# The value products of an attention group issued in one or two bursts in place of three parts

## The reference, cut to what matters

```
sim  = einsum('bhid,bjd->bhij', q, k) * SCALE + attn_bias
sim  = where(causal or masked, -big, sim)
attn = softmax(sim, axis=-1)
out  = einsum('bhij,bjd->bhid', attn, v)      # the value products
out  = ln(out.reshape(b, n, H * DH) @ Wout, g_out)
```

## Time and profile before

| | |
|---|---|
| median of 3 runs | 2250.94 us (2246.36 to 2251.7) |
| span of the profiled execution | 2243.8 us |
| difference of the two | 7.1 us |
| PE busy | 1965.3 us, 88% |
| DVE busy | 1693.1 us, 75% |
| ACT busy | 1338.8 us, 60% |
| POOL busy | 1085.5 us, 48% |

### The profile page before, as it was taken

How to read it: one execution, slowest core, us unless ns; L and a number is a source line. 1 busy time by engine, 2 the same in 40 slices (tenths; PEclk the granted TensorE clock), 3 DMA queues, 4 the chain that set the end, 5 groups by cost and what they waited for, 6 DMA issues and landing times. The chain is left out here.

```text
span 2243.8 us, 46782 instructions
## 1 busy us (share of the span) xinstructions
PE 1965.3 (88%) x11698; PEld 1421.4 (63%) x11698; DVE 1693.1 (75%) x4092; ACT 1338.8 (60%) x2911; POOL 1085.5 (48%) x1307
## 2 busy tenths in 40 slices
PE   5999585999999998589999999985796999999988
PEld 4887463666666668566666666675564666666658
DVE  4777867877887785758777877758577888877857
ACT  2222665777776674247676767644565777766754
POOL 0443222666765562306666666623034666666643
PEclk8999697999999999799999999997896999999999
DMA  4630166333333343286777888830464433333333
GB/s 118 203 109 31 42 226 250 104 113 113 113 114 113 106 149 110 82 312 189 236 241 236 244 244 243 271 142 21 148 229 163 131 115 116 108 115 107 107 113 113
DMA packets 220535, 338.75 MB, mean 151 GB/s; under 512 B 25766, under 2 KB 102700, under 8 KB 220364
## 3 DMA queue, kind: packets, MB, share of 16 engines
q1 hardware_dynamic: 220364, 336.85, 47.3%
HBM read 250.62 MB, written 102.91 MB: 158 GB/s over the span
## 5 line engine op out<-in xcount | busy, mean ns | idle before, releaser
L1653 POOL TENSOR_SCALAR at_row<-at_row,at_inv 128x129 f32<-128x129 f32 (+7 forms) x384 | 715.2, 1862 | 352.9 <-DVE at_inv L1817 347.2
L1864 ACT ACTIVATE at_row<-at_row,at_nmax 128x129 f32<-128x129 f32 (+7 forms) x768 | 595.4, 775 | 231.8 <-DVE at_nmax L1836 230.2
L1836 DVE CUSTOM_DVE_ANT_0 at_row<-at_s,bias,at_row 128x128 f32<-128x128 f32 (+7 forms) x768 | 617.8, 810 | 63.3 <-PE at_s L1764 35.9
L1776 PE MATMUL at_t<-ident,at_row 128*128 128x128 f32 x3456 | 543.9, 280 | 42.6 <-ACT at_pt L1857 37.7
L1776 PEld LDWEIGHTS at_t<-ident,at_row 128*128 128x128 f32 x3456 | 391.4, 141 | 247.9 <-issue 165.7
L1763 PE MATMUL at_s<-k_hh,q_hl 128*128 128x512 f32 (+3 forms) x1152 | 462.2, 401 | 41.9 <-SPq L1721 21.8
L1792 PE MATMUL at_o<-at_pt,v 128*64 128x512 f32 (+3 forms) x2304 | 438.9, 503 | 5.8 <-ACT at_pt L1857 2.5
L1668 DVE COPY at_pt<-at_t 128x128 f32<-128x128 f32 (+3 forms) x576 | 278.5, 484 | 179.6 <-PE at_t L1776 175.7
L1764 PE MATMUL at_s<-k_lp,q_h 65*128 65x512 f32 (+3 forms) x1152 | 392.9, 353 | 0.0
L1857 ACT ACTIVATE at_pt<-at_t 128x512 f32<-128x512 f32 (+2 forms) x576 | 306.7, 533 | 135.5 <-PE at_t L1776 130.3
L1763 PEld LDWEIGHTS at_s<-k_hh,q_hl 128*128 128x128 f32 x1152 | 224.6, 195 | 76.1 <-DVE at_nmax L1836 32.2
(11 more groups left out here) (249 smaller groups left out, 2863.9 us busy)
## 6 DMA issues: line engine op xcount, KB each, us to landing
q_hl<-q_dram SPq DMA_DIRECT2D x192, 256.0 KB, 4.0
q_dram<-o_in SPq DMA_DIRECT2D x76, 512.0 KB, 3.7
bias<-bands_dram SPq DMA_DIRECT2D x64, 512.0 KB, 5.4
q_h<-q_dram SPq DMA_DIRECT2D x96, 256.0 KB, 4.8
o_dram<-o_sb SPq DMA_DIRECT2D x96, 256.0 KB, 4.3
bands_dram<-brow_dram SPq DMA_DIRECT2D x2, 8192.0 KB, 33.6
bias<-corners_dram SPq DMA_DIRECT2D x256, 64.0 KB, 4.2
bias<-in_fside SPq DMA_DIRECT2D x32, 448.0 KB, 4.8
```

The costliest lines, as they stand in the source:

```text
L1653: return eng.tensor_scalar(cells, cells, inv[:, i:i + 1], None, ALU.mult)
L1776: last = eng.transpose(t_ps[m % NTR][:, c * P:(c + 1) * P], row[:, u % RING, here:here + P], t["ident"][:])
L1836: eng.tensor_tensor_reduce(out=row[:, u % RING, ZERO:ZERO + width], in0=s_ps[u % 2][:, 0:width], in1=bt[:, lo:lo + width], scale=-1.0, sca ...
L1864: eng.activation(cells, cells, ACT.Exp, scale=-1.0, bias=nmax[:, i:i + 1], accum_out=rsum[:, i:i + 1]).then_inc(s["exp"], 1)
```

## The change

The steps at which V stands now depend on the parity of the group. An early group's products are issued in one burst at u % 8 = 1. A late group's are issued in two, at u % 8 = 0 and 3, with 8 products each. The step of O follows the last part by one, as it did before.

```diff
-    VALUES_AT = (0, 2, 4)
+    VALUES_AT = ((1,), (0, 3))
@@ values
-                    n = len(VALUES_AT)
+                    n = len(VALUES_AT[g % 2])
@@ TensorE step
                     g = u // GU - 1
-                    if u % GU in VALUES_AT and has(g, NGRP):
-                        values(turn, g, VALUES_AT.index(u % GU))
+                    if u % GU in VALUES_AT[g % 2] and has(g, NGRP):
+                        values(turn, g, VALUES_AT[g % 2].index(u % GU))
@@ ScalarE step
-                    g, part = divmod(n - LAG - VALUES_AT[-1] - 1 - GU, GU)
-                    if part == 0 and has(g, NGRP):
+                    u = n - LAG
+                    g = u // GU - 1
+                    if u % GU == VALUES_AT[g % 2][-1] + 1 and has(g, NGRP):
                         output(turn, g)
```

## The result

The changed kernel took 2308.1 us, the median of 4 runs (2306.52 to 2311.12), against 2249.35 (2246.36 to 2251.7) for the kernel before beside it: a ratio of 1.0258, with a 95% interval of 1.0239 to 1.0277. It is 58.75 us slower. The forecast was 29 us slower, and the time lies 2 us above its range. The direction was right and the size was half.

The account below looks back on a forecast made before the run. TensorE was taken to bound only parts of the period, VectorE being late from A(10) on. 48 periods x (29.1 - 28.49) = +29 us gave span 2273; adding 7.1 to reach the median of the runs gave 2280 us, range 2232 to 2306.

Parts of the forecast that it names:

- Fewer switches: On TensorE, three value-product parts fewer a period at 0.3 us each: 0.9 us saved if TensorE is the bound throughout.
- VectorE's chain: VectorE's additions and scalings from A(10) on: A(13) starts at 16.84, not 15.92, so VectorE is 0.9 us later.
- TensorE's pace: Rival: TensorE sets the pace throughout, 2208 us, or 2231 with half given back; chance 0.22.
- The late group's second burst delays A(10); N(8) meets GpSimd: Behind L(9): VectorE's A(10) starts at 10.76, not 9.35; its scaling N(8) ends at 13.2, not 12.8.
- The early burst delays T(10) and X(15): Behind L(15): T(10) starts at 21.45, not 18.29; ScalarE's X(15) at 22.61, not 20.64, with O ahead of it.
- N(14): "I take 29.1": VectorE's scaling near the period's end: period 29.33 us if slow, 28.9 if quick, 29.1 taken.
- The ordinary period: The schedule laid out from a period without disturbance, 27.92 us before: 29.33 us if N(14) is slow.
- Loop and layer 2: Periods with the loop's branch or layer 2's query wait: waits covered except some 0.45 us; 29.1 taken, between 28.5 and 29.8.
- rival on the clock: Rival: new stands at L(13) to L(15) lower TensorE's clock in each of 24 turns, +36 on top, 2316 us; chance 0.04.
- The sum: Whole kernel: 48 x (29.1 - 28.49) = +29 us, predicted time 2280 us.
- all slow and the branch not covered: Rival: 29.8 us in every period, +63, 2314 us; chance 0.06.
- The page's lock: Rival: at N(14) GpSimd's port lock fully blocks VectorE, twenty-four at 1.2 us, +29 on top, 2309 us; chance 0.02.

Follow-up runs that it names:

- two and two: Kernel before, with two bursts per group: the late group's at 0 and 4, the early group's at 0 and 2; 2229.72 us, ratio 0.9893.
- the short N(9): Changed kernel, with GpSimd's scaling N(9) cut from 641 columns to 129 in every period; 2289.24 us, ratio 1.017.
- 129-column N(15): Changed kernel, with GpSimd's scaling N(15) cut from 1025 columns to 129 in every period; 2274.65 us, ratio 1.0109.

## Why the prediction was half right

- *Fewer switches, 0.9 us a period of TensorE.* Not borne out. The group of the value products is busy 0.76 a period less, but TensorE's whole busy time fell by 3.7 us, 0.08 a period (the rest was overlap counted in two groups). With two and two, two parts fewer, it fell by 15.3 us, 0.16 a part and not 0.3. The forecast didn't rest on this term, since it took VectorE's chain for the limit, and that was right: TensorE's pace as a rival falls with 91% busy and 111.8 us of waits ahead of the logits. Where the parts are fewer and the chain isn't delayed (two and two) the ordinary period of layer 3 is 0.42 shorter.
- *The late group's second burst delays A(10); N(8) meets GpSimd.* Right: 10.81 against 10.76, and N(8) ends at 13.25 against 13.2. Moving that burst by one step gave back 49 us; taking away N(8)'s meeting alone (the short N(9)) gave back 18.
- *The early burst delays T(10) and X(15).* Right in its times. The text lets O stand at the head of ScalarE's queue, and it does; but O one step later brought only 0.1 for X(15), so the hold is T(10) behind the burst.
- *N(14): "I take 29.1".* **This is the step that failed: the length of the period, taken as 29.1 and measured as 29.76 on average.** The mechanism was right and this term too small, in three parts, of which N(14) is one and the next two points are the others. The text gave 29.33 if slow and 28.9 if quick, and the forecast went half way between. The schedule itself had N(14) 0.05 behind GpSimd's start, and the earlier trace rows have a slow one at 0.03 behind. It had to be taken as slow. Measured, it is 0.14 behind in most periods and slow in 42 of 48, and the two cases lie 0.5 apart in the kernel before, near the forecast's 0.43. Taking 29.33 would have added 0.23 x 48 = 11 us.
- *The ordinary period.* With N(14) slow it was forecast at 29.33; the ordinary ones have a mean of 29.58. Steps of 0.05 to 0.12 that add up to T(13), and some periods that are longer still, make 0.25, another 12 us over 48 periods.
- *"Loop and layer 2 … for these I take 29.1 too".* The turn-first periods have a mean of 29.94 (before 29.17), 0.36 above the ordinary ones, which is 0.18 over all. The text itself left some 0.45 of the branch uncovered and then took 29.1 for these periods too, so it put that at nothing. The wait for queries did go, as forecast, and with it layer 2's stretches at the lower clock. Nearly all of the excess lies in the six periods with a stop ahead of C(8), and most of it in two of layer 1, of 32.06 and 31.91 us. In these two, in both kernels, N(12) meets GpSimd's N(13) and takes 1.45 in place of 0.70; in the changed kernel T(12) then starts 1.2 to 1.4 later than in the other two of layer 1 with the stop, and the granted clock is at the lower level (0.50) for 3.4 us. The clock of that layer is 0.99 in the windows, where it was 1.00. That is part of the rival on the clock, at two places in place of 24. Why the clock fell only there stays open.
- *The sum.* 0.23 + 0.25 + 0.18 = 0.66 us a period over 29.1, 32 us in 48. The medians differ by 58.75 and the spans by 65.5: the span of the change's profiled execution lies 1.2 us above the median time, that of before 5.6 below, so that the rows show some 7 us more than the runs.
- *The rival "all slow and the branch not covered".* It came nearest, with 29.8 a period and 2314 us, and had a chance of 0.06. The N(14) are slow in 42 of 48, and the turn-first periods are 0.36 longer, near the 0.45 that the text had left uncovered, though nearly all of it lies in six of them.
- *The page's lock.* By the rule in the Trainium skill's page SBUF — State Buffer (section SBUF: two separate sides), that the loser of the shared port fully blocks for the whole instruction, N(14) would not have ended before 2.9 us behind GpSimd's start. It ended 1.66 behind, so the trace goes against this form of the rule, and the rival built on it falls. What it says of a conflict between the two engines is borne out: with GpSimd's instruction cut short, N(14) took 0.78.

How the 59 us are made up is shown by the runs with parts: 19 for the early burst and 26 for the late ones by themselves, some 14 only for both. In the changed kernel the second late burst at its step is worth 49, of which N(8)'s meeting is 18; that the other 31 are A(10)'s late start by itself is argued from the times in the table, and no run shows it alone.

## What to carry to other kernels

Merging parts of an engine's work can save its switches only where that engine sets the pace, and the saving is read from the engine's whole busy time, not from that of one group: look at what the next engine waits for behind each place, and put a long burst where its follower has slack. Where a schedule laid out by hand ends in a case of two outcomes, take the outcome that its own start times select, not the middle. Whether VectorE or GpSimd pays for a conflict can hang on the difference of two start times (0.028 and 0.030 us here), so count how often it falls each way over all periods, before and after, rather than reading one.

## What the runs showed of the hardware

- **VectorE behind GpSimd is held for a fixed share, and released before GpSimd is done.** Over the 96 periods of the two kernels, N(14) takes 0.74 to 0.76 us wherever it starts from 0.21 ahead of GpSimd's N(15) to 0.028 behind it, and GpSimd's then takes 3.30 to 3.46 in place of 2.90. From 0.030 to 0.22 behind it takes 1.44 to 1.63, and ends 1.66 behind GpSimd's start each time, whether it started 0.05, 0.14 or 0.22 behind. (Of four starts further ahead than 0.21, three took 0.84, 1.62 and 1.85.) It is held for about 1.66 - 0.75 = 0.91 us, 31% of GpSimd's 2.90. For N(8), 641 columns, it is 1.14 - 0.55 = 0.59, 31% of 1.89; an N(8) that starts 0.83 us or more behind takes its 0.55 undisturbed.
- **GpSimd can pay even when it starts first.** The 129-column N(15) starts 0.14 us ahead of VectorE's N(14) and takes 1.06 us, where 129 columns take 0.61 in N(1) of the same run; VectorE's takes 0.78, nearly its undisturbed 0.75.
- **Waiting for the engine's own result costs 0.16 us** where the instruction that makes it stands right in front: VectorE is idle for 60.1 us ahead of 384 scalings behind their reciprocals, and for only 1.3 us in the changed kernel, where a copy stands between.
- **An engine's groups overlap.** In the changed kernel the transposes, the logits and the value products of attention are busy 1556 us added up and 1314 together; before it was 1594 and 1317. So a group that gets shorter needn't make its engine less busy.
